# Layer norm's gain and bias of the first mixture applied by token in two VectorE passes, and high parts rounded straight out of PSUM

## The chip, the cores and the metric

The kernel runs on one core of a Trainium2 chip. The metric is the device time of one execution in microseconds (us); less is better. The profile of the kernel before is one execution recorded by the hardware profiler.

## The reference, cut to what matters

Six layers run one after another on `x` of 4096 tokens by 256 features: mixture 0, attention 0, mixture 0 again, mixture 1, attention 1, mixture 1 again. The change touches mixture 0, which is called twice, as the first and the third layer:

```python
x = x + 0.5 * _L0_ffn_ref(_layernorm(x, axis=-1), ln_g, ln_b, Wr, W1, W3, W2, W1s, W3s, W2s)

def _L0_ffn_ref(x, ln_g, ln_b, Wr, W1, W3, W2, W1s, W3s, W2s):
    h = _layernorm(x, ln_g, ln_b).reshape(Tn, D)     # (x - mu) * rsqrt(var + eps) * g + b
    logits = h @ Wr                                  # 7 experts, the best 2 per token
    ...
    a = jnp.einsum('ecd,edf->ecf', xe, W1)           # xe: up to 732 tokens per expert, rows of h
    b = jnp.einsum('ecd,edf->ecf', xe, W3)
    ye = jnp.einsum('ecf,efd->ecd', jax.nn.silu(a) * b, W2)
    ...
    shared = jax.nn.silu(h @ W1s) * (h @ W3s) @ W2s
    out = routed + shared
```

The gain `g` and the bias `b` have 256 values each, one per feature.

## The kernel before

Every matrix product is made of three: an operand is split in a high part, rounded to the matmul's short format by a copy (ACT), and a low part, the full value less the high part (DVE). `mm3` (L160 to L162) issues high by high, low by high, high by low.

Mixture 0 is the class `Ffn0`. Its work is a list of items written out in `order`, and each engine walks the whole list and issues its own part of each item, in that order; semaphores tie the parts together. An engine never goes past an item that it still waits for.

The tokens lie in 32 tiles of 128. `stats` and `root` make mean (`MV`) and reciprocal deviation (`R`); `norm` writes the normalised rows into `Z`, token on the partition (L212, one DVE `tensor_scalar` of 128x256 per tile: subtract the mean, multiply by the deviation's reciprocal). `zput` stores `Z` to `zn_scratch`, from where the experts' tokens are gathered later (`xr`). `tp` and `xt` turn four tiles (`tp`, 512 tokens) or three gathered ones (`xt`, 366 slots) with TensorE so that the feature is on the partition. There are 16 `tp` and 28 `xt` in a call. Turned, the gain and the bias are one value per partition, and ACT applies them on the way out of PSUM into a buffer, `AUX` (L543, signal `aa`). A second ACT pass rounds that to the high part (L553, signal `fh`), and DVE subtracts for the low part (L628, signal `al`).

All of `tp` (from the third group of tokens on), `lg` (the router's logits, L497), `xt` and a few others share PSUM bank 3 and take turns in it. TensorE waits before each use until the one before has been read: after a `tp` or `xt` that is the signal `aa`. For the first two groups `tp` has banks 4 to 7, and `SIL` and `PROD` stand in for `AUX`.

The shared expert comes first, in steps: `up` of two halves (12 matmuls of 512 columns each), then `down` of the step before (24 of 256 columns). For each half `up` ACT makes the silu (L520), DVE the product (L594), ACT its high part (L524), DVE the low part (L597). `wt` splits weights, once in two steps (L530 ACT, L602 DVE). Into the gaps between them, numbered slots, three to a step, `order` sets the other items. Slot 3s is behind the first half of step s, 3s+1 behind its second half, 3s+2 behind the `down`. This part of it sets the rest of the first three units:

```python
for h in range(2, 8):
    s0 = 9 + 3 * (h - 2)
    for k in range(2):
        slots[s0 - 3 + k].append(("norm", n, 4 * h + 2 * k, 4 * h + 2 * k + 2))
    slots[s0 + 1].append(("zput", n, h))
    slots[s0].append(("tp", n, h, 0))
    slots[s0 + 1].append(("tp", n, h, 1))
    lg_at = s0 + 5 if h < 7 else s0 + 3
    slots[lg_at].append(("lg", n, h))
    if h % 2:
        slots[lg_at + 1].append(("best", n, h // 2))
```

`best` picks each token's experts (DVE L640, L644) and stands ahead of `tp` in slots 13, 18 and 24. At the head of a call two `norm` items of four tiles each come before anything that TensorE can multiply, except `fill` (L169), matmuls of ones that only keep TensorE busy.

The first call is about 700 us long. The constants come at its start from the SP queue (L815, L817): `Wr`, and `g` and `b` as two values per partition.

Of the kernel before, what the change touches and what calls it, by code (L numbers as in the profile page):

```python
# [5 lines left out]
F32 = mybir.dt.float32  # L6
# [3 lines left out]
ALU = mybir.AluOpType  # L10
ACT = mybir.ActivationFunctionType
# [218 lines left out]
class Ffn0:  # L230
# [18 lines left out]
    def __init__(self, chip, call, first):  # L249
# [10 lines left out]
        self.AUX = c.place("AUX", [128, 512])  # L260
# [38 lines left out]
        users = [it for it in self.items if it[0] in ("tp", "xt")]  # L299
        self.aux_before = dict(zip(users[1:], users))  # L300
# [106 lines left out]
    def pe(self, e, w, it):  # L407
# [60 lines left out]
        elif k in ("tp", "lg", "tot", "pos", "xt"):  # L468
            early = k == "tp" and it[2] < 2
            pb = c.bank(4 + 2 * it[2] + it[3] if early else 3)  # L470
            if it in self.bank_before and not early:
                before = self.bank_before[it]
                w.wait_ge(*p.at("aa" if before[0] in ("tp", "xt") else "ad", before))
# [34 lines left out]
    def act(self, e, w, it):  # L508
# [22 lines left out]
        elif k in ("tp", "xt"):  # L531
            early = k == "tp" and it[2] < 2
            h, cc = it[2:] if k == "tp" else divmod(it[3], 2)
            nh = 512 if k == "tp" else 366
            if early:
                src, full = c.bank(4 + 2 * h + cc), (self.PROD if h else self.SIL)[:, cc, :]
            else:
                src, full = c.bank(3, nh), self.AUX[:, 0:nh]
                if it in self.aux_before:
                    w.wait_ge(*p.at("al", self.aux_before[it]))  # L540
            w.wait_ge(*p.at("ax", it))
            w.wait_ge(*p.at("gb", ("consts", n)))
            e.activation(full, src, ACT.Identity, bias=c.GB[:, 1, cc:cc + 1],  # L543
                         scale=c.GB[:, 0, cc:cc + 1]).then_inc(*p.one("aa"))
            w.wait_ge(*p.mine())
# [7 lines left out]
            e.activation(dst, full, ACT.Copy).then_inc(*p.one("fh"))  # L553
# [3 lines left out]
        elif k == "yo":  # L557
# [4 lines left out]
            for t in range(4):  # L562
                e.activation(self.YO[e_ % 2][0:122, t, :], self.slots(t), ACT.Copy,  # L563
                             scale=self.GI[0:122, 6 * e_ + t:6 * e_ + t + 1]).then_inc(*p.one("yo"))

# [8 lines left out]
    def dve(self, e, w, it):  # L574
# [37 lines left out]
        elif k == "norm":  # L612
            w.wait_ge(*p.mine())
            for i in range(it[2], it[3]):
                ins = c.normalise(e, self.Z[:, i, 0:D], i)
            ins.then_inc(*p.one("z"))
        elif k in ("tp", "xt"):
            h, cc = it[2:] if k == "tp" else divmod(it[3], 2)
            w.wait_ge(*p.at("fh", it))
            if k == "tp":  # L620
                early = h < 2
                full = (self.PROD if h else self.SIL)[:, cc, :] if early else self.AUX[:, :]
                hs = slice(512 * (h % 2), 512 * (h % 2) + 512)
                hi, lo = self.FH[h // 2][:, 0, cc, hs], self.FH[h // 2][:, 1, cc, hs]
            else:
                full, hs = self.AUX[:, 0:366], slice(366 * h, 366 * h + 366)
# [2835 lines left out]
```

## Time and profile before

| | us |
|---|---|
| median of 3 runs | 3002.39 (3000.92 to 3003.87) |
| the profiled execution, its own time | 3010.5 |
| its span, first to last instruction | 3008.5 |
| PE busy (matmul) | 2833.7 |
| DVE busy | 1851.9 |
| ACT busy | 1640.4 |

PE is TensorE, DVE is VectorE, ACT is ScalarE, SP is the engine that issues most loads. `Lnnn` is the line of the kernel that issued an instruction. A busy time counts an instruction from its start to its end. Instructions of one engine overlap a little, so that two of 0.41 us each take 0.75 together. "PEclk" is the granted clock of TensorE as a share of full speed: 1.00 is 2.4 GHz, 0.50 is 1.2 GHz. Times in rows are counted from the span's start.

### The profile page before, as it was taken

What the parts mean: (1) busy time and instruction counts of PE and PEld (TensorE: products, weight loads), DVE (VectorE), ACT (ScalarE), POOL (GpSimd) and SP (SyncE); (2) the same over time, 40 slices, a digit from 0 to 9 for tenths busy, and PEclk for the clock granted to TensorE, in tenths of its full rate; (3) what the DMA queues carried; (4) which work ended last, traced back from release to release, by engine and by line L of the source; (5) the groups of instructions that cost most, each with busy time, mean ns of one, the idle gap of its engine ahead of it and who ended that gap; (6) DMA issues with size and microseconds to landing.
All of it is one profiled execution on the core that took longest, in us unless ns stands there. A gap on an engine that the chain in (4) does not pass through costs nothing.

```text
span 3008.5 us, 53567 instructions
## 1 busy us (share of the span) xinstructions
PE 2833.7 (94%) x21877; PEld 2209.6 (73%) x21877; DVE 1851.9 (62%) x3742; ACT 1640.4 (55%) x2467; POOL 547.3 (18%) x479
## 2 busy tenths in 40 slices
PE   8999999997999989999999978997999999997998
PEld 6888999996767678889999946985433434333898
DVE  7675555548877675755555477885535463436776
ACT  4434454543443444344555424775787877891676
POOL 0002223221000000022332254563000000001343
PEclk9999999999999999999999989998999999997999
DMA  4213333332000022133333344773442342513675
GB/s 137 82 56 104 87 94 89 84 80 74 2 3 23 3 64 76 59 102 87 95 88 84 79 143 135 205 194 89 95 127 51 90 88 60 120 36 113 173 202 145
DMA packets 238197, 279.62 MB, mean 93 GB/s; under 512 B 24131, under 2 KB 219392, under 8 KB 237952
## 3 DMA queue, kind: packets, MB, share of 16 engines
q1 hardware_dynamic: 205648, 228.78, 26.3%
q0 software_dynamic: 30720, 45.85, 8.0%
q8 instruction: 172, 2.82, 0.4%
q10 hardware_dynamic: 1584, 1.57, 0.2%
q14 instruction: 73, 0.60, 0.1%
HBM read 204.61 MB, written 72.88 MB: 92 GB/s over the span
## 4 chain that ended last, share of the span: by engine, by line
PE 68%; DVE 16%; issue 4%; ACT 4%; POOL 4%; DMA 3%; DVEq 0%; another core or an unknown queue 0%; POOLq 0%; SPq 0%; ACTq 0%
PE PS L2895 15%; PE PS L160 14%; PE PS L162 14%; PE PS L161 14%; PE PS L993 6%; DMA GR<-xn_scratch,SM 2%; POOL xa_scratch L2338 1%; DVE SM L185 1%; DVE PROD L594 1%; ACT FW L530 1%; PE PS L497 1%; DVE FHH L597 1%; DVE FW L602 1%; ACT FHH L524 1%; ACT Z L563 1%
## 5 line engine op out<-in xcount | busy, mean ns | idle before, releaser
L3044 ACT ACTIVATE P<-PS 128x1024 f32<-128x1024 f32 x512 | 487.7, 1041 | 108.3 <-PE PS L2895 106.1
L160 PE MATMUL PS<-FH,FW 128*128 128x366 f32 (+1 forms) x1408 | 510.4, 363 | 14.6 <-ACT SIL L520 6.1
L161 PE MATMUL PS<-FH,FW 128*128 128x366 f32 (+1 forms) x1408 | 501.9, 356 | 0.0
L162 PE MATMUL PS<-FH,FW 128*128 128x366 f32 (+1 forms) x1408 | 500.3, 355 | 0.0
L524 ACT ACTIVATE FHH<-PROD 128x366 fp32r<-128x366 f32 (+1 forms) x352 | 195.9, 556 | 544.1 <-DVE PROD L594 518.8
L597 DVE TENSOR_TENSOR FHH<-PROD,FHH 128x366 fp32r<-128x366 f32 (+1 forms) x352 | 209.9, 596 | 219.3 <-ACT FHH L524 218.7
L160 PE MATMUL PS<-FW,FHH 128*122 128x256 f32 (+1 forms) x1184 | 339.0, 286 | 1.8 <-DVE FHH L597 1.7
L161 PE MATMUL PS<-FW,FHH 128*122 128x256 f32 (+1 forms) x1184 | 333.2, 281 | 1.0 <-issue 1.0
L162 PE MATMUL PS<-FW,FHH 128*122 128x256 f32 (+1 forms) x1184 | 333.1, 281 | 0.0
L594 DVE TENSOR_TENSOR PROD<-SIL,PS 128x366 f32<-128x366 f32 (+1 forms) x352 | 207.0, 588 | 159.2 <-PE PS L162 139.0
L160 PEld LDWEIGHTS PS<-FH,FW 128*128 128x128 f32 x1408 | 267.2, 190 | 39.6 <-ACT SIL L520 10.7
L162 PEld LDWEIGHTS PS<-FH,FW 128*128 128x128 f32 x1408 | 268.8, 191 | 22.4
L161 PEld LDWEIGHTS PS<-FH,FW 128*128 128x128 f32 x1408 | 267.2, 190 | 18.0 <-issue 0.7
L2895 PE MATMUL PS<-P,V 128*32 128x512 f32 x2048 | 275.0, 610 | 2.5 <-DVE OC L3191 2.0
L602 DVE TENSOR_TENSOR FW<-WST,FW 128x1536 fp32r<-128x1536 f32 x96 | 168.8, 1758 | 129.0 <-ACT FW L530 122.1
L520 ACT ACTIVATE SIL<-PS 128x366 f32<-128x366 f32 (+1 forms) x352 | 180.9, 514 | 120.4 <-PE PS L162 119.7
L800 POOL DMA_INDIRECT xa_scratch<-Z,RV x84 | 140.3, 1670 | 537.4 <-ACT Z L563 484.7
L160 PEld LDWEIGHTS PS<-FW,FHH 128*122 128x122 f32 (+1 forms) x1184 | 220.7, 186 | 5.9 <-DVE FHH L597 2.8
L161 PEld LDWEIGHTS PS<-FW,FHH 128*122 128x122 f32 (+1 forms) x1184 | 220.8, 187 | 3.2 <-issue 1.3
L162 PEld LDWEIGHTS PS<-FW,FHH 128*122 128x122 f32 (+1 forms) x1184 | 220.7, 186 | 0.5 <-issue 0.5
L790 POOL DMA_INDIRECT Z<-zn_scratch,RV x84 | 95.9, 1142 | 573.1 <-DVE RV L764 486.4
L2895 PE MATMUL PS<-S,S 64*128 64x512 f32 x1024 | 193.4, 453 | 1.0 <-DVE S L3185 1.0
(454 smaller groups left out, 5633.9 us busy)
## 6 DMA issues: line engine op xcount, KB each, us to landing
WS<-L_ffn_w_dram SPq DMA_DIRECT2D x256, 256.0 KB
WST<-L_ffn_W_dram SPq DMA_DIRECT2D x168, 256.0 KB
S<-parts_scratch SPq DMA_DIRECT2D x60, 384.0 KB, 8.0
parts_scratch<-PT SPq DMA_DIRECT2D x28, 512.0 KB, 3.8
WST<-L_ffn_W1s_dram SPq DMA_DIRECT2D x40, 256.0 KB
WST<-L_ffn_W3s_dram SPq DMA_DIRECT2D x40, 256.0 KB
WST<-L_ffn_W2s_dram SPq DMA_DIRECT2D x40, 256.0 KB
xa_scratch<-X SPq DMA_DIRECT2D x17, 512.0 KB, 5.5
```

The costliest lines, as they stand in the source:

```text
L160: e.matmul(o, lh, rh, start=start, stop=False, skip_group_check=True)
L161: e.matmul(o, ll, rh, start=False, stop=False, skip_group_check=True)
L162: return e.matmul(o, lh, rl, start=False, stop=stop, skip_group_check=True)
L520: e.activation(self.SIL[:, h, 0:NH], c.bank(2 * self.up_at[it] % 3, NH), ACT.Silu).then_inc(*p.one("sil"))
L524: e.activation(self.FHH[:, s % 2, 0, hs], self.PROD[:, h, 0:NH], ACT.Copy).then_inc(*p.one("hi"))
L594: e.tensor_tensor(self.PROD[:, h, 0:NH], self.SIL[:, h, 0:NH], c.bank((2 * self.up_at[it] + 1) % 3, NH), ALU.mult).then_inc(*p.one("mul"))
L597: e.tensor_tensor(self.FHH[:, s % 2, 1, hs], self.PROD[:, h, 0:NH], self.FHH[:, s % 2, 0, hs].bitcast(F32), ALU.subtract).then_inc(*p.one( ...
L602: e.tensor_tensor(self.FW[:, q % 2, 1, :], self.WST[:, q % 2, :], self.FW[:, q % 2, 0, :].bitcast(F32), ALU.subtract).then_inc(*p.one("wo"))
L800: e.indirect_dma_start(out=c.XA, out_offset=bass.IndirectOffsetOnAxis(ap=self.TO.bitcast(U32)[:, 6 * e_ + t:6 * e_ + t + 1], axis=0), in_= ...
L993: mm = lambda o, l, r, a=True, z=True: e.matmul(o, l, r, start=a, stop=z, skip_group_check=True)
L2895: mm = lambda o, l, r, a=True, z=True: e.matmul(o, l, r, start=a, stop=z, skip_group_check=True)
L3044: e.activation(self.PR[K % 3][:, 2 * jj:2 * jj + 2, :].rearrange("p a b -> p (a b)"), c.pair(2 * ((2 * K + jj) % 3)), ACT.Exp, scale=0.25) ...
```

## The change

`GB` (gain and bias, one value per partition) goes. `GAIN` and `BIAS` are rows of 256 values, the same in every partition, in the place of `AUX`; each is filled by a load of 1 KB per partition, 128 KB in all. `norm` makes two passes over its tiles: first all of them, (x - mean) * gain, then all of them, times the deviation's reciprocal, plus bias. The second waits for the first. `norm` now waits for `gn`, the arrival of gain and bias. `Z`, and so `zn_scratch`, holds the finished rows. ACT's pass to `AUX` goes, 44 per call; the high part is rounded from PSUM, and the low part is taken by DVE from PSUM too. So a `tp` or `xt` frees bank 3 only when DVE has read it: the wait of the bank's next user is for `al`.

```diff
-        "tp": {"ax": 1, "aa": 1, "fh": 1, "al": 1}, "lg": {"ax": 1, "ad": 1},
+        "tp": {"ax": 1, "fh": 1, "al": 1}, "lg": {"ax": 1, "ad": 1},
...
-        self.AUX = c.place("AUX", [128, 512])
+        self.GAIN, self.BIAS = c.place("GAIN", [128, 256]), c.place("BIAS", [128, 256])
...
-                w.wait_ge(*p.at("aa" if before[0] in ("tp", "xt") else "ad", before))
+                w.wait_ge(*p.at("al" if before[0] in ("tp", "xt") else "ad", before))
...
-            if early:
-                src, full = c.bank(4 + 2 * h + cc), (self.PROD if h else self.SIL)[:, cc, :]
-            else:
-                src, full = c.bank(3, nh), self.AUX[:, 0:nh]
-                if it in self.aux_before:
-                    w.wait_ge(*p.at("al", self.aux_before[it]))
-            w.wait_ge(*p.at("ax", it))
-            w.wait_ge(*p.at("gb", ("consts", n)))
-            e.activation(full, src, ACT.Identity, bias=c.GB[:, 1, cc:cc + 1],
-                         scale=c.GB[:, 0, cc:cc + 1]).then_inc(*p.one("aa"))
-            w.wait_ge(*p.mine())
+            src = self.turned(it)
...
-            e.activation(dst, full, ACT.Copy).then_inc(*p.one("fh"))
+            e.activation(dst, src, ACT.Copy).then_inc(*p.one("fh"))
...
+    def turned(self, it):
+
+        if it[0] == "tp" and it[2] < 2:
+            return self.c.bank(4 + 2 * it[2] + it[3])
+        return self.c.bank(3, 512 if it[0] == "tp" else 366)
...
             w.wait_ge(*p.mine())
+            w.wait_ge(*p.at("gn", ("consts", n)))
             for i in range(it[2], it[3]):
-                ins = c.normalise(e, self.Z[:, i, 0:D], i)
+                ins = e.scalar_tensor_tensor(self.Z[:, i, :], c.X[:, i, :], c.MV[:, i, 0:1], self.GAIN[:, :], ALU.subtract,
+                                             ALU.mult)
+            ins.then_inc(*p.one("dv"))
+            w.wait_ge(*p.mine())
+            for i in range(it[2], it[3]):
+                ins = e.scalar_tensor_tensor(self.Z[:, i, :], self.Z[:, i, :], c.R[:, i:i + 1], self.BIAS[:, :], ALU.mult,
+                                             ALU.add)
             ins.then_inc(*p.one("z"))
...
-            e.tensor_tensor(lo, full, hi.bitcast(F32), ALU.subtract).then_inc(*p.one("al"))
+            e.tensor_tensor(lo, self.turned(it), hi.bitcast(F32), ALU.subtract).then_inc(*p.one("al"))
...
-                e.dma_start(c.GB[:, x, :], A[f"L0_ffn_ln_{name}"].rearrange("(c p) -> p c", p=128),
-                            allow_slow_non_contiguous=True).then_inc(*p.dma("gb"))
+                e.dma_start((self.BIAS if x else self.GAIN)[:, :], A[f"L0_ffn_ln_{name}"].partition_broadcast(128),
+                            allow_slow_non_contiguous=True).then_inc(*p.dma("gn"))
```

This is DVE's row of instructions at the head of the first call, from `norm` to the low parts of the first two groups, with the waits that each carries:

```order
-L212 TENSOR_SCALAR Z_72<-X_49,SM_52 128x256 [waits dv]
-L212 TENSOR_SCALAR Z_72<-X_49,SM_52 128x256 x3
-L212 TENSOR_SCALAR Z_72<-X_49,SM_52 128x256 [waits z]
-L212 TENSOR_SCALAR Z_72<-X_49,SM_52 128x256 x3
...
+L609 SCALAR_TENSOR_TENSOR Z_72<-X_49,SM_52,GAIN_81 128x256 [waits gn,dv]
+L609 SCALAR_TENSOR_TENSOR Z_72<-X_49,SM_52,GAIN_81 128x256 x3
+L614 SCALAR_TENSOR_TENSOR Z_72<-Z_72,SM_52,BIAS_82 128x256 [waits dv]
+L614 SCALAR_TENSOR_TENSOR Z_72<-Z_72,SM_52,BIAS_82 128x256 x3
...
+L595 TENSOR_TENSOR FW_77<-WST_86,FW_77 128x1536 [waits wh]
+L626 TENSOR_TENSOR FH_25_73<-PS,FH_25_73 128x512 [waits fh] x4
```

Each `norm` has two groups of instructions in the place of one, the split of the weights and the low parts stand behind them as before, and the low parts now read PSUM (`PS`).

This is TensorE's row of instructions in slots 10 to 14 of the first call, the users of bank 3 alone, of the kernel before: second `tp` of group 2, both of group 3, then `lg` of group 2.

```order
L479 MATMUL PS<-IDENT_50,Z_72 128x128 [waits aa]
...
L479 MATMUL PS<-IDENT_50,Z_72 128x128 [waits z,aa]
...
L479 MATMUL PS<-IDENT_50,Z_72 128x128 [waits aa]
...
L497 MATMUL PS<-WRR_84,FH_26_74 128x16 [waits al,aa]
```

And the same of the changed kernel:

```order
L477 MATMUL PS<-IDENT_50,Z_72 128x128 [waits al]
...
L477 MATMUL PS<-IDENT_50,Z_72 128x128 [waits z,al]
...
L477 MATMUL PS<-IDENT_50,Z_72 128x128 [waits al]
...
L495 MATMUL PS<-WRR_85,FH_26_74 128x16 [waits al]
```

The instructions stand where they stood; each wait for ACT's pass (`aa`) has become one for DVE's subtraction (`al`) of the same item.

## Rows read from the trace of the kernel before

**Rows 1.** The page: span, busy times, and the chain that ended last by engine.

```profile
span 3008.5 us, 53567 instructions
...
PE 2833.7 (94%) x21877; PEld 2209.6 (73%) x21877; DVE 1851.9 (62%) x3742; ACT 1640.4 (55%) x2467; POOL 547.3 (18%) x479
...
PE 68%; DVE 16%; issue 4%; ACT 4%; POOL 4%; DMA 3%; DVEq 0%; another core or an unknown queue 0%; POOLq 0%; SPq 0%; ACTq 0%
```

**Rows 2.** Waits, 30 to 145 us, PE's: total us, times, longest.

```profile
PE PS L479 <- DVE Z L212: 4.1, 2, 2.7
PE PS L497 <- ACT AUX L543: 1.4, 2, 0.8
PE PS L479 <- ACT AUX L543: 1.1, 1, 1.1
```

**Rows 3.** Timeline, head of the first call: start, us, engine, line [idle before].

```profile
11.80 2.80 DVE L212 TENSOR_SCALAR Z<-X,SM 128x256 f32<-128x256 f32 x8
...
18.11 0.47 PE L160 MATMUL PS<-FH,FW 128*128 128x512 f32 x1 [2.36 <-DVE FH L628]
```

**Rows 4.** Groups by line and shape, DVE, 0 to 760 us: busy us, mean ns.

```profile
L212 DVE TENSOR_SCALAR Z<-X,SM 128x256 f32<-128x256 f32 x32 | 11.6, 410 | 0.5
...
L652 DVE TENSOR_TENSOR RT<-RT 128x256 f32<-128x256 f32 x2 | 0.8, 422 | 0.1
...
L594 DVE TENSOR_TENSOR PROD<-SIL,PS 128x512 f32<-128x512 f32 x64 | 43.7, 683 | 35.3 <-PE PS L162 30.0 <-remote 4.4 <-issue 0.9
...
L628 DVE TENSOR_TENSOR FH<-AUX,FH 128x512 fp32r<-128x512 f32 x12 | 8.2, 684 | 4.5 <-ACT FH L553 4.5
```

**Rows 5.** Timeline, DVE, slots 12 and 13 of the first call.

```profile
67.50 0.69 DVE L628 TENSOR_TENSOR FH<-AUX,FH 128x512 fp32r<-128x512 f32 x1 [0.64 <-ACT FH L553]
...
70.98 0.65 DVE L640 MAX8 RT<-RT 128x8 f32<-128x8 f32 x8
...
72.76 0.68 DVE L628 TENSOR_TENSOR FH<-AUX,FH 128x512 fp32r<-128x512 f32 x1
```

**Rows 6.** Timeline, PE, bank 3's users in slots 9, 10, 12, 14 and 19.

```profile
51.12 0.63 PE L479 MATMUL PS<-IDENT,Z 128*128 128x128 f32 x4 [2.66 <-DVE Z L212]
...
54.63 0.66 PE L479 MATMUL PS<-IDENT,Z 128*128 128x128 f32 x4
...
62.38 0.63 PE L479 MATMUL PS<-IDENT,Z 128*128 128x128 f32 x4 [1.48 <-DVE Z L212]
...
70.94 0.61 PE L497 MATMUL PS<-WRR,FH 128*128 128x16 f32 x4 [0.57 <-ACT AUX L543]
...
91.49 0.38 PE L479 MATMUL PS<-IDENT,Z 128*128 128x128 f32 x2
```

**Rows 7.** Timeline, DVE, the low part of slot 18.

```profile
92.36 0.68 DVE L628 TENSOR_TENSOR FH<-AUX,FH 128x512 fp32r<-128x512 f32 x1
```

**Rows 8.** The second call: its start, and PE at slot 9.

```profile
1062.17 0.46 SPq L817 DMA_DIRECT2D SM<-L_ffn_ln_b_dram  x1
...
1063.95 0.41 DVE L212 TENSOR_SCALAR Z<-X,SM 128x256 f32<-128x256 f32 x1
...
1103.32 0.63 PE L479 MATMUL PS<-IDENT,Z 128*128 128x128 f32 x4 [2.58 <-DVE Z L212]
```

**Rows 9.** DMA issues, 1055 to 1075 us: size, us to landing.

```profile
zn_scratch<-Z SPq DMA_DIRECT2D x2, 512.0 KB, 4.5
...
SM<-L_ffn_ln_b_dram SPq DMA_DIRECT2D x1, 1.0 KB, 2.2
```

**Rows 10.** DMA issues, 0 to 12 us.

```profile
SM<-L_ffn_ln_b_dram SPq DMA_DIRECT2D x1, 1.0 KB, 6.8
```

**Rows 11.** Windows: from:to, length, PE, PEld, DVE, ACT, POOL busy, PEclk, DMA share, GB/s.

```profile
48.30:51.10 2.80, 0.17 (x1) 0.01 (x1) 2.69 (x10) 1.57 (x2) 0.00 (x0) 1.00 0.00 0
...
97.60:102.00 4.40, 4.40 (x14) 3.44 (x14) 2.19 (x3) 0.78 (x2) 0.00 (x0) 0.61 0.36 123
...
10.90:13.30 2.40, 0.00 (x0) 0.00 (x0) 2.19 (x10) 1.11 (x1) 0.00 (x0) 1.00 1.09 348
```

More of the change, by code:

```diff
@@ L298, in __init__ @@
         self.bank_before = dict(zip(uses[1:], uses))
-        users = [it for it in self.items if it[0] in ("tp", "xt")]
-        self.aux_before = dict(zip(users[1:], users))
         for it in self.items:
@@ L531, in act @@
         elif k in ("tp", "xt"):
-            early = k == "tp" and it[2] < 2
+            w.wait_ge(*p.at("ax", it))
             h, cc = it[2:] if k == "tp" else divmod(it[3], 2)
-            nh = 512 if k == "tp" else 366
-            if early:
-                src, full = c.bank(4 + 2 * h + cc), (self.PROD if h else self.SIL)[:, cc, :]
-            else:
-                src, full = c.bank(3, nh), self.AUX[:, 0:nh]
-                if it in self.aux_before:
-                    w.wait_ge(*p.at("al", self.aux_before[it]))
-            w.wait_ge(*p.at("ax", it))
-            w.wait_ge(*p.at("gb", ("consts", n)))
-            e.activation(full, src, ACT.Identity, bias=c.GB[:, 1, cc:cc + 1],
-                         scale=c.GB[:, 0, cc:cc + 1]).then_inc(*p.one("aa"))
-            w.wait_ge(*p.mine())
+            src = self.turned(it)
             if k == "tp":
@@ L620, in dve @@
             if k == "tp":
-                early = h < 2
-                full = (self.PROD if h else self.SIL)[:, cc, :] if early else self.AUX[:, :]
                 hs = slice(512 * (h % 2), 512 * (h % 2) + 512)
@@ L625, in dve @@
             else:
-                full, hs = self.AUX[:, 0:366], slice(366 * h, 366 * h + 366)
+                hs = slice(366 * h, 366 * h + 366)
                 hi, lo = self.XT[it[2] % 2][:, 0, cc, hs], self.XT[it[2] % 2][:, 1, cc, hs]
-            e.tensor_tensor(lo, full, hi.bitcast(F32), ALU.subtract).then_inc(*p.one("al"))
+            e.tensor_tensor(lo, self.turned(it), hi.bitcast(F32), ALU.subtract).then_inc(*p.one("al"))
         elif k == "lg":
```

4 rows, old and new, of the table COUNTS are left out of this document.

## The prediction

> **What bounds the kernel now.** I read the page first: PE is busy for 2834 of 3008.5 us, DVE for 1852, ACT for 1640, and the chain that ended last is PE for 68% and DVE for 16% [rows 1]. ACT, from which the change takes 88 passes, has 4% of the chain. So the averages say that a pass less on ACT is worth little and one more on DVE may be hidden. That holds for no single stage, so I asked for the waits of the stage where the touched items stand, the shared expert's first three units (30 to 145 us). There TensorE waits for what the change touches and hardly for anything else: twice for a normalised tile (4.1 us) and three times for ACT to free bank 3 (1.4 and 1.1 us) [rows 2]. The timeline of DVE from 46 to 76 us has no idle time apart from its turns with ACT: PE stands from 48.3 to 51.1 us and again for 1.5 us up to 62.38 because DVE is late with `norm` [rows 6, 11]. DVE bounds this stretch. The second call repeats it, wait for wait (2.58 us at its slot 9) [rows 8]. At the head of a call DVE alone is between the data and the first product: `norm`, the weights' split, the first low parts, and PE waits for the last of them [rows 3].
>
> **The price of one pass.** No row shows a `scalar_tensor_tensor` of 128x256 out of SBUF. The nearest are a `tensor_tensor` of that shape and the `tensor_scalar` it replaces, 422 and 410 ns, as good as equal [rows 4]. Eight of the latter take 2.80 us, so one costs (2.80 - 0.41)/7 = 0.34 us in a row and the last 0.41. I take the same for each new pass. They bound it from below, since a second source can hardly make it cheaper; from above I take the 683 ns of twice the columns. The low part read from PSUM costs what it cost: 683 ns with a PSUM operand, 684 without [rows 4].
>
> The Trainium skill ("VectorE: DVE Perf Modes", the walkthrough of the modes) says that fp32 `tensor_scalar` out of SBUF runs at two results a cycle and an operation with two tensor sources at one, so that each new pass would cost twice the old one. By the rows, 410 against 422 ns, the trace does not agree here; its mechanism is rival 4, with a price from rows.
>
> **The head of each call.** Two `norm` items of four tiles were 2.80 us together. Now they are four groups of four, each 3 x 0.34 + 0.41 = 1.43 us and 0.04 for the semaphore: 5.9 us, 3.1 more. In the first call the chain behind them is all DVE, so the first product moves from 18.1 to 21.2 us: +3.1. ACT's saving in that place is off the path, since DVE gets to the low parts only after the weights. Gain and bias must have arrived: the tiny load of `b` was issued at 2.3 us and took 6.8 us behind the rows of `x` [rows 10], so it landed at 9.1; `norm` starts at 11.80 [rows 3]. The queues move 348 GB/s about then [rows 11], so 256 KB more adds 0.7 us, and the cover of 2.7 us holds. If it were gone, every us past it would count. The weights behind them on SP's queue land 0.7 us later, and DVE now asks for their split 3.1 us later than it did. In the second call there is none: `b` is issued at 1062.17 and `norm` began at 1063.95, 1.8 us later [rows 8], while even 1 KB took 2.2 us to land and 512 KB took 4.5 [rows 9]. That bounds the wait by 0.4 and 2.7 us; between them by size, 128 KB lands after 2.8 us, and I take 1.0. What queues behind it on DVE is the whole head. So the heads cost 3.1 + 4.1 = 7.2 us.
>
> **Slots 6 to 14, worked as a schedule.** Each later `norm` has two tiles: 0.75 us before, now 0.75 + 0.04 + 0.75, 0.79 more. In slots 6 and 7 that makes `Z` late by 1.6 us, and PE's first `tp` starts at 52.7 in place of 51.12 [rows 6]. Its low part then comes on DVE behind a `stats` item, at 57.6 to 58.3. Before, PE put the second `tp` into bank 3 at 54.63, as soon as ACT had read it [rows 6]. Now it must wait for DVE until 58.3, +3.7. That is absorbed, because PE's next wait is for `norm` again: two more pairs in slots 9 and 10 make 4 x 0.79 = 3.2 us, and PE starts at 65.5 for 62.38 [rows 6]. In slot 12 DVE gains: it idled 0.64 us for ACT's second pass [rows 5], which now is over before the low part of the product is, so its low part is +2.5; one `norm` makes +3.3. Then in slot 13 `best` (70.98 to 72.76) stands ahead of the low part [rows 5], which is +3.3 too and ends at 76.8. `lg` in slot 14 took the bank at 70.94, when ACT had read it [rows 6]; now it waits for that end: **+5.9 us**. That is the largest new wait, and the instructions queued behind it on PE are the matmuls of the next step.
>
> **Slots 15 to 26.** From here DVE had idle time and PE hardly waited, so the added passes are hidden and PE keeps its +5.9, plus what bank 3 costs. Slot 17: low part ends 0.5 us after PE wants the bank, +6.4. Slot 18 has `best` again: the low part ran from 92.36 to 93.04 [rows 7] while PE's second `tp` stood at 91.49 [rows 6]; 1.6 us, +8.0. Slot 20 adds nothing, as DVE has its 0.64 us back. Slot 23 is as slot 17, 0.7 us, +8.7. Slot 25, behind the third `best`, is as slot 18: 1.6, **+10.3**. After slot 26 nothing of the change is left on the path. The experts' 28 `xt` lie one to a step, each many us from bank 3's next user, and PE does not wait there for ACT's pass, so dropping it gives nothing. What PE has lost it does not win back, since DVE idles there, waiting for PE. Two calls: 2 x 10.3 = 20.6 us, of which 2 x 3.3 is the second pass and 2 x 7.0 the later release of the bank.
>
> **The clock.** The granted clock was 0.61 from 97.6 to 102.0 us, a mean over both levels, 2.4 and 1.2 GHz, right after the router's thin matmuls of 16 columns; 4.4 x (1 - 0.61) = 1.7 us of PE's work were lost there [rows 11]. Longer stands ought to bring more of that. How many more no row tells: none is one bound, three in each call (10 us) the other. PE's stand of 2.8 us at 48.3 went with a clock of 1.00 [rows 11]; it becomes 4.4 us. I take one more stretch in each call, 2 x 1.7 = 3.4 us.
>
> The Trainium skill ("TensorE: Matmul & The Clock Gate", § What's actually happening) says that idle time returns the array to 1.2 GHz. The trace agrees in part: the fall comes, but the stand of 2.8 us had none.
>
> **Sum.** 7.2 + 20.6 + 3.4 = 31.2 us. The profiled execution would have a span of 3008.5 + 31 = 3039; its own time of 3010.5 lies 8 above the median of the runs. On the median of 3002.4 I add the same 31.2 and get 3034.
>
> **The rivals.**
>
> 1. *The bank costs nothing*: if DVE took the low parts sooner than my schedule has it, only the second pass would count: 7.2 + 6.6 + clock 0 to 3.4, so 3016 to 3020. For it speaks that 3.7 us were absorbed in slot 10; against it that `best` stands ahead of three low parts by the order.
> 2. *The clock falls often*: two or three new stretches in each call in place of one, 3037 to 3041, and with stretches that last twice as long 3044.
> 3. *Faster*: the second pass is hidden in DVE's idle time and the waits for ACT's second pass go, 7 x 0.64 = 4.5 us in each call, all of it on the path: 2993. It needs DVE to have idle time where PE waits for `norm`; it decides if the wait at 62.38 is released by something other than L212. The timeline shows DVE without a gap there.
> 4. *A pass costs 0.27 us more* (683 for 410 ns), if two tensor sources slow a pass. The 16 passes of each head make 4.3 us, the 20 up to slot 12 make 5.4, together 2 x 9.7 = 19.4 more, 3053. With all 48 passes behind the head on the path (13 us in place of 5.4) it is 3069. Against it stand the 422 ns.
> 5. *No change*: passes and waits are all covered. The head alone speaks against it.
>
> **How the numbers follow.** The forecast, 3034 with 3027 to 3040 as its own range, has 0.70; rival 2, 0.13; rival 1, 0.11; rival 4, 0.03; rival 3, 0.01; rival 5, 0.02. A difference under 0.2%, 6 us, is about what a measurement of this kernel can't tell from none. Leaving out rivals 3 to 5 and the far ends of 1 and 2, the range is 3018 to 3044. All of the first three are slower by over 0.2%: 0.97; same 0.02, faster 0.01.
>
> **What the profile after would show.** Step by step: L609 and L614 at 0.41 us, their groups of four 1.43 us. First product at about 21.2 us. In the second call 1 us of idle before the first L609, put down to a load. PE's waits between 30 and 160 us: for L614 in slots 9 and 12, and for L626 in slots 10, 13, 14, 18 or 19, and 25, of which the one before `lg` in slot 14 is the longest felt. DVE idle before L626 near zero. No difference in length from 300 to 650 us. I would be wrong if a pass takes other than 0.34 us in a row, if DVE caught up within slots 6 to 14, or if PE regained time in the steps behind.

## The result, and the profile after

The changed kernel takes 3037.85 us (median of 5, 3036.76 to 3045.3) against 3000.92 us of the kernel before (median of 5, 2999.68 to 3003.87) on the same chip: 1.0126 times as long, 95% interval 1.0112 to 1.014. That is 37 us slower. The forecast was 3034 in 3018 to 3044, and 31 us slower.

The page of the kernel after (its own time 3039.83 us), which answers to [rows 1]: span, busy times, chain.

```profile
span 3038.1 us, 53439 instructions
...
PE 2841.2 (94%) x21877; PEld 2216.4 (73%) x21877; DVE 1877.9 (62%) x3806; ACT 1576.8 (52%) x2379; POOL 547.0 (18%) x479
...
PE 67%; DVE 17%; issue 4%; ACT 4%; DMA 4%; POOL 4%; DVEq 0%; POOLq 0%; SPq 0%; ACTq 0%
```

ACT is relieved of 64 us, DVE has 26 more, and PE's busy time is up by 7.5 us where the span is up by 29.6: most of the new time is idle time of PE. Its waits, 30 to 160 us (total, times, longest), answer to [rows 2]:

```profile
PE PS L477 <- DVE Z L614: 5.9, 2, 4.8
PE PS L495 <- DVE FH L626: 5.1, 4, 2.8
PE PS L477 <- DVE FH L626: 4.7, 3, 1.8
PE PS L500 <- DVE RT L650: 0.7, 1, 0.7
```

ACT has gone from this list, and DVE has 15.7 us of it where it had 4.1: 5.9 for normalised tiles, 9.8 for bank 3 (L626, the low part). (The wait for `RT`, 0.7 us, is in the kernel before too and not counted.) The new passes by line and shape, DVE, 0 to 760 us (busy us, mean ns, idle before), as in [rows 4]:

```profile
L614 DVE SCALAR_TENSOR_TENSOR Z<-Z,SM,BIAS 128x256 f32<-128x256 f32 x32 | 13.9, 482 | 0.5
L609 DVE SCALAR_TENSOR_TENSOR Z<-X,SM,GAIN 128x256 f32<-128x256 f32 x32 | 13.9, 482 | 0.5
L626 DVE TENSOR_TENSOR FH<-PS,FH 128x512 fp32r<-128x512 f32 x16 | 10.6, 679 | 0.0
```

A pass takes 482 ns, not 410, and the idle time before the low part (4.5 us in [rows 4]) is 0.0. The head of the first call, timeline of DVE and then PE, beside [rows 3]:

```profile
12.17 1.67 DVE L609 SCALAR_TENSOR_TENSOR Z<-X,SM,GAIN 128x256 f32<-128x256 f32 x4
13.88 1.67 DVE L614 SCALAR_TENSOR_TENSOR Z<-Z,SM,BIAS 128x256 f32<-128x256 f32 x4
...
22.47 0.77 PE L160 MATMUL PS<-FH,FW 128*128 128x512 f32 x1 [1.48 <-DVE FH L626]
```

Four passes in a row take 1.67 us, so one costs (1.67 - 0.48)/3 = 0.40 us in a row. The head of the second call has a wait that was not there before:

```profile
1082.95 1.67 DVE L609 SCALAR_TENSOR_TENSOR Z<-X,SM,GAIN 128x256 f32<-128x256 f32 x4 [1.01 <-DMA BIAS<-L_ffn_ln_b_dram]
```

The users of bank 3 in slots 9, 12, 13, 14, 17, 19 and 25, timeline of PE, which answers to [rows 6]:

```profile
57.81 1.09 PE L477 MATMUL PS<-IDENT,Z 128*128 128x128 f32 x4 [4.76 <-DVE Z L614]
...
71.20 0.63 PE L477 MATMUL PS<-IDENT,Z 128*128 128x128 f32 x4 [1.13 <-DVE Z L614]
76.33 0.66 PE L477 MATMUL PS<-IDENT,Z 128*128 128x128 f32 x4 [1.76 <-DVE FH L626]
...
82.64 2.03 PE L495 MATMUL PS<-WRR,FH 128*128 128x16 f32 x16 [2.78 <-DVE FH L626]
...
96.24 1.97 PE L495 MATMUL PS<-WRR,FH 128*128 128x16 f32 x16 [0.68 <-DVE FH L626]
...
107.29 0.66 PE L477 MATMUL PS<-IDENT,Z 128*128 128x128 f32 x4 [1.47 <-DVE FH L626]
...
134.77 0.66 PE L477 MATMUL PS<-IDENT,Z 128*128 128x128 f32 x4 [1.48 <-DVE FH L626]
```

For all comparisons below I cut an execution at marks of the timeline: the *head* of a call of mixture 0 (from the span's start, or from the second call's first `fill`, to the first product L160), its *front* (from there to the end of the last `lg`), and the rest. Two executions of the kernel before are given, since one is no measure of the spread; the second is the first experiment. "Stood" is the length of a front less PE's busy time in it (fills count as busy). "Lost" is the length of a front times (1 - PEclk), with PEclk worked out from the trace to five digits, since the two digits of a window leave 0.6 us open over such a length. All in us, from one profiled execution each.

| kernel | head 1, 2 | front 1, 2 | PE stood in front 1, 2 | lost in front 1, 2 | both heads and fronts | all the rest | span |
|---|---|---|---|---|---|---|---|
| before | 18.1, 10.6 | 109.8, 110.1 | 6.9, 6.8 | 6.83, 6.83 | 248.6 | 2759.9 | 3008.5 |
| before, again | 18.2, 9.2 | 106.7, 106.6 | 5.5, 5.5 | 5.12, 5.12 | 240.6 | 2750.1 | 2990.7 |
| after | 22.5, 16.7 | 122.4, 120.9 | 15.7, 16.8 | 10.47, 6.83 | 282.4 | 2755.7 | 3038.1 |
| passes alone | 22.2, 16.4 | 119.9, 116.5 | 11.6, 12.9 | 12.16, 6.83 | 275.0 | 2758.8 | 3033.8 |
| bank alone | 18.3, 10.4 | 113.6, 109.4 | 9.5, 9.2 | 8.21, 3.41 | 251.7 | 2757.1 | 3008.8 |
| `best` behind | 22.2, 16.1 | 122.0, 120.3 | 13.2, 13.8 | 13.43, 10.24 | 280.6 | 2752.8 | 3033.4 |
| more fills | 22.0, 14.7 | 122.6, 121.6 | 12.7, 13.6 | 9.10, 6.83 | 280.9 | 2755.1 | 3036.0 |

The rest, which the change doesn't touch, is 2750 to 2760 us in every kernel, those of before among them, and moves by itself. All that the change costs lies in heads and fronts: +33.8 us against the one execution of before, +41.8 against the other. The medians say 36.9, between the two.

### The profile page after: what moved, and what is told of

It is laid out like the page before. It is cut to its first block, busy times and chain, and to the rows that moved or that the text cites. A ratio compares the mean times of both kernels' runs of the same rounds, so it can differ in the third digit from the quotient of the medians.

```text
span 3038.1 us, 53439 instructions
## 1 busy us (share of the span) xinstructions
PE 2841.2 (94%) x21877; PEld 2216.4 (73%) x21877; DVE 1877.9 (62%) x3806; ACT 1576.8 (52%) x2379; POOL 547.0 (18%) x479
## 4 chain that ended last, share of the span: by engine, by line
PE 67%; DVE 17%; issue 4%; ACT 4%; DMA 4%; POOL 4%; DVEq 0%; POOLq 0%; SPq 0%; ACTq 0%
PE PS L2893 14%; PE PS L160 14%; PE PS L161 13%; PE PS L162 13%; PE PS L991 6%; DMA GR<-xn_scratch,SM 2%; POOL xa_scratch L2336 1%; DVE SM L185 1%; DVE FHH L590 1%; DVE PROD L587 1%; ACT FHH L522 1%; PE PS L495 1%; ACT FW L528 1%; DVE FW L595 1%; ACT Z L550 1%
## 5 line engine op out<-in xcount | busy, mean ns | idle before, releaser
L160 PE MATMUL PS<-FH,FW 128*128 128x366 f32 (+1 forms) x1408 | 512.4, 364 | 11.3 <-ACT SIL L518 6.0
L160 PE MATMUL PS<-FW,FHH 128*122 128x256 f32 (+1 forms) x1184 | 338.9, 286 | 1.5 <-DVE FHH L590 1.5
L160 PEld LDWEIGHTS PS<-FH,FW 128*128 128x128 f32 x1408 | 269.1, 191 | 36.1 <-ACT SIL L518 10.6
L161 PEld LDWEIGHTS PS<-FH,FW 128*128 128x128 f32 x1408 | 268.6, 191 | 18.2 <-issue 0.7
L160 PEld LDWEIGHTS PS<-FW,FHH 128*122 128x122 f32 (+1 forms) x1184 | 221.1, 187 | 4.9 <-DVE FHH L590 1.9
```

The source lines that it names most:

```text
L160: e.matmul(o, lh, rh, start=start, stop=False, skip_group_check=True)
L161: e.matmul(o, ll, rh, start=False, stop=False, skip_group_check=True)
```

## The experiments

**1. The kernel before, profiled once more.** No edit.

> The kernel before, once more. Its profiled execution had a span of 3008.5 us, while its timed runs are at 3000 to 3004; the changed kernel's profile (3038.1) agrees with its runs. If that one profile of before was a slow one by chance, this span is 2999 to 3003 and the missing 6 to 8 us lie in stages that the change doesn't touch (attention 0, the experts). If runs and profiles of before always differ so, it is about 3008 again.

One execution took 2992.69 us, span 2990.7: 18 us less than the execution of [rows 1], 8.0 of them in heads and fronts and 9.8 in the rest. Neither guess was met: it lies 8 us below the nearer one, and nearly half of the difference is in stages that the change does touch. So a difference of spans between two single profiles is uncertain by some 18 us here. From here on the medians are compared, and the profiles stage by stage.

**2. The two passes alone.** The two passes in `norm` as in the changed kernel; ACT copies to `AUX` again (without scale and bias, which are in the rows already) and frees the bank by `aa`. `GAIN` and `BIAS` lie in a part of `RT` that is not yet used.

```diff
-        self.GAIN, self.BIAS = c.place("GAIN", [128, 256]), c.place("BIAS", [128, 256])
+        self.AUX = c.place("AUX", [128, 512])
+        self.GAIN, self.BIAS = cut(RT, 1480, 256), cut(RT, 1736, 256)
...
-                w.wait_ge(*p.at("al" if before[0] in ("tp", "xt") else "ad", before))
+                w.wait_ge(*p.at("aa" if before[0] in ("tp", "xt") else "ad", before))
...
+            e.activation(full, src, ACT.Copy).then_inc(*p.one("aa"))
...
-            e.tensor_tensor(lo, self.turned(it), hi.bitcast(F32), ALU.subtract).then_inc(*p.one("al"))
+            e.tensor_tensor(lo, full, hi.bitcast(F32), ALU.subtract).then_inc(*p.one("al"))
```

> The two passes of norm alone: gain and bias are applied by token, but ACT still copies bank 3 to AUX first and TensorE gets the bank at that copy's end, as before. Main theory: the heads cost what they cost in the changed kernel (4.4 and 6.1 us with the wait for the loads), and behind them 4 x 1.05 us until slot 12, one more 1.05 in slot 13 before the router's matmul and one in slot 19, 6.3 us in each call. Together 10.5 + 12.6 = 23 us slower than before, down to 18 if some is won back in the units behind. Rival, the bank's later release does it all behind the heads: 11 us. Rival, the passes do it all: 30 us or more.

Measured: 3035.55 us (3034.06 to 3041.49) against 3003.05, ratio 1.0124 (1.0108 to 1.014), so +32.5 us. That is more than the 18 to 23 of the main guess; the second rival's figure, 30 us or more, is what came. The passes alone make nearly the whole loss. (ACT's copy without scale and bias took 0.58 us here, 0.76 with them in the kernel before, so the bank comes free a little sooner than it did.) PE's waits, 30 to 160 us:

```profile
PE PS L480 <- DVE Z L620: 7.1, 2, 4.8
PE PS L498 <- ACT AUX L543: 3.1, 3, 1.8
PE PS L498 <- DVE RT L639: 1.2, 1, 1.2
```

The stand of 4.8 us for the first later tile is the same as in the changed kernel, and with the bank freed by ACT the long one before `lg` is shorter. But the waits for ACT are 3.1 us where they were 2.5 [rows 2]: ACT too comes late. One of them, timeline of ACT and then PE, the router's `lg` in slot 20, in the kernel before and then here:

```profile
94.45 0.63 ACT L524 ACTIVATE FHH<-PROD 128x512 fp32r<-128x512 f32 x1 [2.80 <-DVE PROD L594]
94.99 0.76 ACT L543 ACTIVATE AUX<-PS,SM 128x512 f32<-128x512 f32 x1
...
95.80 1.95 PE L497 MATMUL PS<-WRR,FH 128*128 128x16 f32 x16 [0.85 <-ACT AUX L543]
```

```profile
106.34 0.63 ACT L525 ACTIVATE FHH<-PROD 128x512 fp32r<-128x512 f32 x1 [4.04 <-DVE PROD L593]
106.88 0.58 ACT L543 ACTIVATE AUX<-PS 128x512 f32<-128x512 f32 x1
...
107.51 1.95 PE L498 MATMUL PS<-WRR,FH 128*128 128x16 f32 x16 [1.75 <-ACT AUX L543]
```

ACT's copy out of the bank stands in ACT's row behind the high part of DVE's product, and DVE's product stands behind `norm`. So the added passes delay the bank even where DVE doesn't free it.

**3. The bank alone.** One `norm` pass as before, the high part straight out of PSUM and the bank freed by the low part, as in the changed kernel. Gain and bias are left out of the computation.

```diff
-            w.wait_ge(*p.at("gn", ("consts", n)))
...
-                ins = e.scalar_tensor_tensor(self.Z[:, i, :], c.X[:, i, :], c.MV[:, i, 0:1], self.GAIN[:, :], ALU.subtract,
-                                             ALU.mult)
...
+                ins = c.normalise(e, self.Z[:, i, 0:D], i)
```

> The straight rounding out of PSUM alone: norm is one pass as before, gain and bias are left out of the computation (ACT's pass to AUX is gone, bank 3 is freed by DVE's low part). The two loads stay but nothing waits for them. Main theory: heads as before; slot 12 +0.7, slot 14 +1.9 us behind best, slots 19 and 25 +1.6 each less 0.85 that was a wait for ACT, in sum 4.2 us in each call, 8.4 us slower than before. Rival, it is a gain by itself because ACT's pass and DVE's waits for it (4.5 us a call) go: 5 to 9 us faster. Rival, bank release costs 7 us a call also without the second pass: 14 us slower.

Measured: 3009.12 us (3004.09 to 3011.7) against 3003.05, ratio 1.0022 (1.0012 to 1.0033), +6.1 us, where 8.4 was the main guess; the interval leaves out both rivals, the gain and the 14 us. Timeline of PE in slots 9 and 10:

```profile
52.62 0.63 PE L477 MATMUL PS<-IDENT,Z 128*128 128x128 f32 x4 [2.64 <-DVE Z L212]
58.23 0.76 PE L477 MATMUL PS<-IDENT,Z 128*128 128x128 f32 x4 [2.21 <-DVE FH L619]
```

The wait for the bank is there (2.21 us in slot 10), yet the two fronts together, 223.0 us, are only 3.1 and 9.8 us above the two executions of before. In this call the wait for `norm` in slot 12, 1.48 us in [rows 6], is gone: the wait in slot 10 has taken its place. The sum of experiments 2 and 3, 38.6 us, is close to the 36.9 of both.

**4. `best` behind the low part.** The changed kernel with `best` set behind `norm` and `tp` in slots 13, 18 and 24.

```diff
+        for s in (13, 18, 24):
+            slots[s].sort(key=lambda it: it[0] == "best")
```

> The changed kernel with best set behind tp and norm in slots 13, 18 and 24, so that the low part that frees bank 3 doesn't queue behind it. Main theory: the waits of TensorE for L626 at the router's matmul in slot 14 (2.8 us), in slot 19 (1.5) and in slot 25 (1.5) lose 1.8, 1.5 and 1.5 us: 4.8 us a call, 9.6 us faster than the changed kernel, some 27 us slower than before by the timed runs. Rival, DVE is behind anyway and another wait takes over: no faster than the changed kernel (37 us slower than before).

Measured: 3038.94 us (3035.12 to 3044.07) against 3003.05, ratio 1.0131 (1.0115 to 1.0146). Nothing was won, as the rival had it. PE's waits, 30 to 160 us:

```profile
PE PS L479 <- DVE Z L616: 6.1, 2, 4.8
PE PS L497 <- DVE FH L628: 5.3, 5, 2.6
PE PS L479 <- DVE FH L628: 1.8, 1, 1.8
```

The waits of transposes for the bank fell from 4.7 to 1.8 us as intended, and PE stood 5.4 us less in the two fronts. But they lost more to the clock, 13.43 and 10.24 us in place of 10.47 and 6.83. So 6.4 us went there, and the fronts are shorter by only 0.9 us in all. (That the one brought the other is a reading, not shown.)

**5 to 7. More fills.** If idle time of PE costs a second time through its clock, matmuls of ones in the idle time give that part back. The changed kernel with more `fill` at the heads and ahead of the waits for `norm` in slots 9 and 12:

```diff
-        seq += [("norm", n, i, i + 4) for i in (0, 4)] + [("wrr", n), ("wt", n, 0), ("fill", n, 8 if self.first else 2)]
-        seq += [("tp", n, h, c) for h in range(2) for c in range(2)] + [("fill", n, 0 if self.first else 3)]
+        seq += [("norm", n, i, i + 4) for i in (0, 4)] + [("wrr", n), ("wt", n, 0), ("fill", n, 12 if self.first else 7)]
+        seq += [("tp", n, h, c) for h in range(2) for c in range(2)] + [("fill", n, 1 if self.first else 1)]
...
+                if it[2:] in ((2, 0), (3, 0)):
+                    c.fill(e, w, 3, 4 if h == 2 else 1)
```

> The changed kernel with matmuls of ones in TensorE's stands: 12 in place of 8 at the first head, 7 in place of 2 at the second and 1 in place of 3 behind its transpositions, 1 in place of none there in the first call, and 4 and 1 ahead of the waits for norm in slots 9 and 12 (stands of 4.8 and 1.1 us). Main theory: the stands are set by VectorE and stay, but the clock that they lower comes back: from the changed kernel's windows, 1 - PEclk times length is lost to it, 3.1 us in head 1, 11.0 behind it, 5.2 in head 2, 7.3 behind it; a third to a half of that (9 to 13 us) comes back, about 25 us slower than before. Rival, the clock has no part in it: within 3 us of the changed kernel.

The same with `best` behind:

> The same fills and best behind tp and norm. With best behind tp alone the stands fell by some 3.3 us a call, while 1 - PEclk times length rose by 2.4 and 3.5 us. Main theory: with the clock held up the shorter stands show: 5 to 9 us faster than with the fills alone. Rival, the order of best has no effect on the end: the same as with the fills alone within 2 us.

And the kernel before with such fills (10 and 4, then 0 and 1 at the heads, 2 and 1 in the slots):

> The kernel before with fills in its own stands: 10 in place of 8 and 4 in place of 2 ahead of the transpositions, 1 in place of 3 behind them in the second call, 2 and 1 ahead of the waits for norm in slots 9 and 12 (2.7 and 1.5 us). Main theory: it gains what the clock lost there, less than in the changed kernel because its stands are shorter: 3 to 8 us faster than before. Rival, no difference, or 2 to 3 us slower because the fills end after the tiles are ready.

Measured against 2999.52 us: changed kernel with fills 3035.91 (3033.54 to 3037.71), ratio 1.0118 (1.0103 to 1.0134); with `best` behind as well 3031.6 (3024.5 to 3036.54), 1.0109 (1.0091 to 1.0127); kernel before with fills 2998.14 (2995.53 to 3001.75), 0.9997 (0.9988 to 1.0006). None of the three main guesses came: the first and the third are no different from their kernels without fills, and the second lies just under its 5 to 9 us. The fills did raise the clock where they stand: 0.86 to 0.95 in head 1, 0.69 to 0.88 in head 2, which became 2.0 us shorter. The fronts did not become shorter. What the first products got, windows of PE from the first product on, changed kernel with fills:

```profile
22.00:26.00 4.00, 4.00 (x10) 3.17 (x11) 1.01 (x2) 1.18 (x2) 0.00 (x0) 0.50 0.90 292
```

The clock is at its lower level, 1.2 GHz (PEclk 0.50), for these 4 us, although five fills more stood ahead of them. There the test didn't do what it was made for. In slot 9 it did. The window behind the wait for `norm` has a clock of 1.00 (the changed kernel without these fills had 0.51 there, below), and PE's next `tp`, in slot 10, then waits for the low part (window, then timeline of PE; the second call repeats both, with 2.31 us):

```profile
57.50:64.00 6.50, 4.18 (x23) 3.35 (x24) 5.70 (x12) 1.60 (x3) 0.00 (x0) 1.00 0.23 81
```

```profile
63.22 0.66 PE L479 MATMUL PS<-IDENT,Z 128*128 128x128 f32 x4 [2.30 <-DVE FH L628]
```

So in that slot the low clock had only filled time in which PE would have stood, and the front is no shorter without it. Such fills give 2.0 us at one head and nothing in the fronts; what the low clock costs in the other slots they do not say. Setting `best` behind, beside the same fills, brought 4.3 us by the medians with intervals that overlap; by the profiles the fronts are equal (122.6 + 121.6 and 120.6 + 123.2). That stays inconclusive.

**8 and 9. `norm` off DVE.** If DVE's row is what sets the front, the kernel before must gain when something leaves that row. The kernel before, with `norm` of tiles 8 to 31 (24 of 32) on GpSimd:

```diff
-        elif k == "norm":
+        elif k == "norm" and it[2] < 8:
...
+        elif k == "norm" and it[2] >= 8:
+            w.wait_ge(*p.at("nr", ("root", n, 8, 16) if it[2] < 16 else ("root", n, 16, 32)))
+            for i in range(it[2], it[3]):
+                ins = c.normalise(e, self.Z[:, i, 0:D], i)
+            ins.then_inc(*p.one("np"))
```

> The kernel before with norm of tiles 8 to 31 on GpSimd, idle there, where the same instruction takes 1.2 us in another stage in place of 0.41. If VectorE's work in slots 6 to 14 is what TensorE waits for, taking 12 x 0.75 us off it shortens the stands for norm (4.1 us a call) and those for ACT's pass (2.5): 8 to 13 us faster than before in both calls together, by the same rule by which the second pass makes it slower. Rival, VectorE is not the bound and its added passes only shift waits: no difference. A third way: GpSimd slows VectorE's instructions at its side, seen in their durations, and the gain is lost.

Measured: 2988.94 us (2983.41 to 2992.16) against 2999.52, ratio 0.996 (0.9947 to 0.9974): 10.6 us faster, **faster than both kernels**. A second time, beside experiment 10:

> The kernel before with norm of tiles 8 to 31 on GpSimd, a second time, as the ground for the run beside it: 10 us faster than before again, ratio 0.996, if that gain is of the kernel and not of the day; 0.999 or more if it was.

2991.53 us (2987.24 to 2992.91) against 3002.46, ratio 0.996 (0.9946 to 0.9973): 10.9 us again. The group on GpSimd and PE's waits, first measurement, 30 to 160 us:

```profile
L212 POOL TENSOR_SCALAR Z<-X,SM 128x256 f32<-128x256 f32 x24 | 31.9, 1342 | 48.9 <-DVE SM L208 48.9
```

```profile
PE PS L481 <- ACT AUX L545: 2.9, 2, 1.6
PE PS L160 <- DVE PROD L596: 1.3, 1, 1.3
PE PS L499 <- DVE RT L635: 1.1, 1, 1.1
```

A pass takes 1342 ns there on the mean, three times DVE's 410, and the waits for `norm` are gone all the same. The fronts are 102.2 and 101.2 us (102.7 and 103.0 in the second measurement), for 110 and 107 before. DVE's operations beside it, 30 to 122 us, before and then with GpSimd: number and shortest/median/longest in ns of one line, and the group of another. The second fence has GpSimd's passes as well:

```profile
L597 DVE TENSOR_TENSOR FHH<-PROD,FHH x16: 691/692/693, 35.1 to 119.2; 128x512 fp32r<-128x512 f32 x16
...
L602 DVE TENSOR_TENSOR FW<-WST,FW 128x1536 fp32r<-128x1536 f32 x4 | 7.0, 1747 | 0.0
```

```profile
L599 DVE TENSOR_TENSOR FHH<-PROD,FHH x17: 691/693/996, 35.0 to 119.5; 128x512 fp32r<-128x512 f32 x17
...
L212 POOL TENSOR_SCALAR Z<-X,SM x24: 1210/1216/2734, 38.2 to 82.6; 128x256 f32<-128x256 f32 x24
...
L604 DVE TENSOR_TENSOR FW<-WST,FW 128x1536 fp32r<-128x1536 f32 x5 | 8.7, 1742 | 0.7 <-ACT FW L532 0.7
```

The mean of L599, 731 ns for 692 before, hides what happened. GpSimd ran `norm` from 38.2 to 48.2 and from 61.9 to 83.9 us. Seven of DVE's 17 L599 fall in there; four of them took 691 to 693 ns as ever, three took 872, 874 and 996. GpSimd paid more: its pass took 1216 ns as a rule and 2734 once, and that one began 0.1 us after a split of weights on DVE (L604, 1.75 us). The Trainium skill ("Perfetto Trace Analysis", § Optimizing Scalar/DVE Operations) warns that the two engines share a read port and that moving work between them might not help. The trace agrees that they disturb each other, by 0.7 us on DVE's L599 and some 3 us on GpSimd in these 92 us; but GpSimd had time to spare, and the move brought 10.6 us.

**10. The bank alone, with `norm` off DVE.** Experiment 3 with the edit of experiment 8 (gain and bias left out of the computation again).

> The kernel with one pass and the bank freed by the low part, gain and bias left out of the computation, and with norm of tiles 8 to 31 moved to GpSimd. Theory (the later release of the bank costs because VectorE's queue is full in slots 6 to 14, and norm is part of it): with norm away from it, the low parts come in time but for the slots where best stands ahead of them, so the two rules of release differ by less than they did: 0 to 3 us slower than the kernel before with norm on GpSimd, ratio to before 0.996 to 0.998. Rival (the release costs by itself, by ACT's pass and VectorE's behind it): the 6 us that it cost beside the kernel before are there again, ratio 0.9985.

Measured: 3004.99 us (2990.43 to 3009.28) against 3002.46, ratio 1.0002 (0.999 to 1.0015), so 13.5 us more than the run beside it without the bank's edit. The rival held, and more: the later release costs not less without `norm` in DVE's row but more, 13.5 us by the medians for the 6.1 of experiment 3. (The intervals of the two differences overlap, so the factor is loose.) Timelines of PE, the users of bank 3 that waited, first with the bank freed by ACT (experiment 9), then by the low part:

```profile
52.19 0.66 PE L481 MATMUL PS<-IDENT,Z 128*128 128x128 f32 x4 [2.01 <-ACT AUX L545]
...
62.88 0.66 PE L481 MATMUL PS<-IDENT,Z 128*128 128x128 f32 x4 [1.23 <-ACT AUX L545]
```

```profile
53.96 0.95 PE L479 MATMUL PS<-IDENT,Z 128*128 128x128 f32 x4 [3.77 <-DVE FH L621]
...
69.61 0.61 PE L497 MATMUL PS<-WRR,FH 128*128 128x16 f32 x4 [1.35 <-DVE FH L621]
...
91.73 0.66 PE L479 MATMUL PS<-IDENT,Z 128*128 128x128 f32 x4 [1.48 <-DVE FH L621]
...
115.55 0.66 PE L479 MATMUL PS<-IDENT,Z 128*128 128x128 f32 x4 [1.46 <-DVE FH L621]
```

These stands are 3.2 us with ACT's release and 8.1 with the other, 4.8 more. The first front of each, windows in the same order:

```profile
18.18:120.91 102.73, 99.29 (x597) 86.97 (x598) 68.10 (x212) 47.76 (x71) 31.99 (x24) 0.97 0.27 89
```

```profile
18.18:125.58 107.40, 99.33 (x597) 87.34 (x598) 67.61 (x212) 36.40 (x56) 31.11 (x24) 0.97 0.27 87
```

PE is busy for the same 99.3 us at the same clock of 0.97, and the front is 4.7 us longer: it is all standing, as counted. The second front grew from 103.0 to 109.1 us. Freeing the bank later costs some 5 to 6 us a call here; where `norm` is in DVE's row PE waits for that anyway, and part of it doesn't show.

## Why the prediction was right, point by point

**The sum.** Forecast +31.2 us, measured +36.9 by the medians (33.6 to 42.0 by the interval of the ratio). The mechanism of the schedule held, and what it fell short by is mostly one term; the shares that I read off it did not hold. Of my three signs of being wrong one came: a pass takes other than 0.34 us in a row.

**The price of a pass: mis-sized.** 0.40 us in a row and 0.48 alone in place of 0.34 and 0.41. A second source made the operation dearer than either row that I took it from, by 60 to 72 ns, though far less than the upper bound of 683. A `norm` of two tiles costs 0.88 + 0.04 + 0.88 = 1.80 us for 0.75, that is +1.05 and not +0.79. The rule of the Trainium skill that I weighed ("VectorE: DVE Perf Modes", the walkthrough of the modes: one tensor source at two results a cycle, two at one) would have made it twice the old pass; the trace has 482 for 410. What doesn't fit the rule is the old pass, not the new one. The kernel before has, in its attention, a `tensor_scalar` of the same shape that multiplies by a constant, and that one takes 284 ns (DVE, 0 to 760 us: busy us, mean ns, idle before):

```profile
L1276 DVE TENSOR_SCALAR SEL<-SM 128x256 fp32r<-128x256 f32 x4 | 0.9, 284 | 0.0
```

So a faster `tensor_scalar` is there to be had; why L212, with two scalars by partition, doesn't get it was not tried.

**The heads: +7.2 forecast, +10.5 measured against the execution of [rows 3].** Four groups of 1.67 us and their semaphores make 6.84 for 2.80 us, +4.0 in each call and not +3.1. In the first call `norm` also started 0.37 us later (12.17 for 11.80) and the product came at 22.47 for 18.11, +4.4. In the second the wait for `BIAS` was 1.01 us, forecast 1.0: there the load landed 3.1 us after its issue, where I had put 2.8. Head 2 grew by 6.1; the 1.1 beyond pass and wait come from fills behind the transposes at a low clock, as far as experiment 5 shows it: with fewer there and more ahead, the head was 2.0 us shorter. Head 2 of the kernel before moves as well, 10.6 and 9.2 us in its two executions.

**Slots 6 to 14: the schedule held, with the dearer pass.** Take off the head's 4.4 us and the rows of before become a test of each step. First later tile: 57.81 for 51.12, +2.3 (forecast 1.6; two pairs at 1.05 make 2.1). Slot 12: 71.20 for 62.38, +4.4 (forecast 3.2; four pairs make 4.2). `lg` in slot 14: 82.64 for 70.94, +7.3 (forecast 5.9). The wait in slot 10 was absorbed as I had said, by the next wait for `norm`; what filled the time there in the first call was a stretch at the lower clock, below, and no stand.

**Slots 15 to 26.** Forecast 0.5, 1.6, 0, 0.7 and 1.6 us in slots 17, 18 or 19, 20, 23 and 25; measured stands 0.68, 1.47, 0.90, 0.70 and 1.48. In slot 20 the kernel before stood 0.85 us for ACT (the line is in experiment 2), so that slot too adds nothing, as forecast. The front ended 16.9 us later in call 1, 12.5 without the head, where 10.3 + 1.7 = 12.0 had been forecast; in call 2 it grew by 10.7. Against the other execution of before the fronts grew by 15.7 and 14.3, so the close fit is partly one of the execution from which the rows were taken.

**The clock.** Forecast 1.7 us per call, measured 3.6 and 0.0 more lost in the fronts of the profiled execution than in that of [rows 11]: 3.6 for 3.4. Against the other execution of before it is 5.4 and 1.7, so the near hit is in part luck. The stretch behind the stand of 4.76 us in slot 9, window of PE (columns as in [rows 11]):

```profile
58.50:64.00 5.50, 5.50 (x16) 4.22 (x15) 4.70 (x12) 1.71 (x3) 0.00 (x0) 0.51 0.28 95
```

5.5 us at 0.51, the lower level of 1.2 GHz, is 2.8 us of work. The kernel before stood 2.8 us there and had 1.00, in the stand [rows 11] and in the matmuls behind it:

```profile
51.10:57.00 5.90, 5.76 (x36) 4.93 (x37) 5.09 (x11) 2.42 (x4) 0.00 (x0) 1.00 0.26 92
```

That is no rule for short stands. In its other execution the same kernel stood 2.63 us there and had 0.66 behind it:

```profile
49.60:54.60 5.00, 4.98 (x18) 4.02 (x19) 4.23 (x10) 2.42 (x4) 0.00 (x0) 0.66 0.32 108
```

Nor did it cost the whole of what it lost: PE's next wait for `norm` was 0.26 us in that execution and 1.48 in [rows 6]. The same holds for the changed kernel: its stretch lies before PE's next waits for DVE and filled time in which it would have stood, as experiment 5 shows, where it is gone and the front no shorter. So of rival 2, call 1 has the amount of two new stretches, call 2 none, and the stretch in slot 9 was free as far as one profile of each kernel tells.

**How the loss was split: this step failed.** I had the second pass hidden from slot 15 on ("DVE had idle time and PE hardly waited"), and so gave 2 x 3.3 us of the fronts to the passes and 2 x 7.0 to the bank. Alone, the passes cost 32.5 us and the bank 6.1. By what PE stood in the table, against the execution of [rows 1], the passes alone add 4.8 and 6.1 us to the fronts, the bank alone 2.7 and 2.4, both 8.8 and 9.9 (forecast 10.3). Against the other execution of before it is 6.1 and 7.4, 4.0 and 3.7, 10.2 and 11.3. So a call has 5 to 7 us from the passes and 2.5 to 4 from the bank, near the reverse of my shares, and the two about add up; neither hides the other. What the runs put in place of the step: the dearer pass explains 1.0 a call (four pairs at 1.05 for 0.79), and behind slot 14 the passes are not hidden, since DVE's product waits behind them, ACT's high part for the product, and ACT's release of the bank behind that (experiment 2). So most of what I charged to the bank's new rule there is lateness of DVE, which the old rule passes on too. The stand of 0.68 us in slot 17 is in neither part alone.

What the bank's edit costs also depends on what else is in the row. With `norm` off DVE it makes 4.7 and 6.1 us, more than beside it. PE waits for the normalised tile in slot 12 anyway, so a late bank in slot 10 is free as long as `norm` is late too: in experiment 3 the one wait took the other's place, in experiment 10 there was none to take. The forecast of the whole was saved by working out both in one schedule, so that an error in the shares could not reach the sum.

**The other rivals.** Rival 1 (3016 to 3020), rival 3 (faster) and rival 5 fell with the medians. Rival 4 had the right direction: 0.07 us more for a pass and not 0.27.

**What stays open.** Why the kernel with `best` behind loses more to the clock though it waits less; it was not tried apart from the order. What the low clock costs outside slot 9: only there does a run hold the work the same and the clock up. What becomes of the two added passes if they go to GpSimd; only the old single pass was moved there. And two executions of one kernel differ by 3.5 us in a front, so shares of 1 us per call taken from one profile are no more than likely.

## What to carry to other kernels

Ask which engine's row of work is full where the touched items stand, not which engine is busy on the average: DVE is busy for 62% of this kernel, with no gap but its turns with ACT where it counts, and no run gained from the passes saved on ACT. When two added delays meet on one engine, lay them out in one schedule, and read no shares off it: the one laid down first gets too little, as the passes did here. A release by another engine is not free of the busy one if its row waits for that engine's results. A wait that is covered by another comes out when the other goes, as it did here when `norm` left DVE. Have two profiles of the kernel before: the fit to one of them, and each rule of the clock read from it, looked firmer here than the second allowed. And price an operation that no row shows with a margin over its nearest rows: 14 to 18% on the passes was 3.9 us (1.8 at the heads, 2.1 in the slots) of the 5.7 that this forecast lacked.

## What the runs showed of the hardware

- `scalar_tensor_tensor` of 128x256 f32 with a scalar by partition and two tensors out of SBUF took 482 ns alone and 0.40 us in a row, where `tensor_scalar` of that size with two scalars by partition took 410, with a constant 284, and `tensor_tensor` 422. On 128x8 and 128x16 it took 0.17 to 0.18 us, as the others.
- Behind the same stand of PE, 2.66 us in one execution of the kernel before and 2.63 in the other, the granted clock was 1.00 over 5.9 us and 0.66 over 5.0 us. Behind one of 4.76 us, in the changed kernel, it was 0.51 over 5.5 us.
- The same 128 KB broadcast to 128 partitions landed after 6.7 and 7.5 us beside the loads of `x`, and after 2.8 and 3.1 us in the second call.
- `tensor_scalar` of 128x256 on GpSimd took 1216 ns as a rule and up to 2734 beside a busy DVE (mean 1342). Of seven `tensor_tensor` of 128x512 on DVE at the same time, four took their usual 691 to 693 ns and three 872 to 996.
